# One loop instead of two: projections and linear attention by token tile, and norms by halves

## The reference

```python
mod = (silu(c) @ wmod)                      # sa, ca, ga, sb, cb, gb
h = layernorm(x) * (1 + ca) + sa
x = x + ga * attn(h)
h = layernorm(x) * (1 + cb) + sb
x = x + gb * ffn(h)
```

```python
q, k, v = x @ Wq.T + bq, x @ Wk.T + bk, x @ Wv.T + bv
g = sigmoid(x @ Wg.T + bg)
q, k = elu(rope(q)) + 1, elu(rope(k)) + 1
S = S + k_chunk.T @ v_chunk;  Z = Z + k_chunk.sum()
out = g * (q_chunk @ S) / (q_chunk @ Z + 1e-6);  y = out @ Wo.T + bo
```

## Time and profile before

| | |
|---|---|
| median of 3 runs | 743.06 us (739.28 to 743.28) |
| the profiled execution | 742.98 us |
| its span, first to last instruction | 741.2 us |
| mean granted TensorE clock | 0.92 of full |
| busy: TensorE, VectorE, ScalarE, GpSimd | 640.0, 478.9, 331.2, 167.9 us |

### The profile page before, as it was taken

One profiled execution on the slowest core, in us unless ns is written; L12 is line 12 of the kernel. 1 busy time (PEld: TensorE's weight loads), 2 busy tenths in 40 slices (PEclk: granted clock), 3 DMA queues, 4 the chain that ended last, 5 costly groups with the idle time before them and its releaser, 6 DMA issues.

```text
span 741.2 us, 10397 instructions
## 1 busy us (share of the span) xinstructions
PE 640.0 (86%) x3825; PEld 415.2 (56%) x3825; DVE 478.9 (65%) x982; ACT 331.2 (45%) x515; POOL 167.9 (23%) x206
## 2 busy tenths in 40 slices
PE   3948967999999959279999999668799999989996
PEld 3846746777777747135544433555454444358885
DVE  6894576777667469677888920476689888233333
ACT  5114043333333332405556676454265666844332
POOL 2451140555555309411000000000010001003222
PEclk9985586999999989569999999899899999999999
DMA  8720140000000000473100000016630000050001
GB/s 249 259 86 1 30 134 1 22 22 21 1 1 0 1 0 1 141 225 107 43 2 2 2 2 1 0 43 181 203 89 2 2 2 2 2 171 1 0 1 57
DMA packets 37182, 39.10 MB, mean 53 GB/s; under 512 B 4046, under 2 KB 36060, under 8 KB 36876
## 3 DMA queue, kind: packets, MB, share of 16 engines
q1 hardware_dynamic: 37132, 38.44, 16.8%
HBM read 30.89 MB, written 7.34 MB: 52 GB/s over the span
## 4 chain that ended last, share of the span: by engine, by line
PE 42%; issue 22%; DVE 12%; POOL 11%; SPq 5%; ACT 3%; DMA 3%; POOLq 0%; DVEq 0%; ACTq 0%
POOL it_lo L1534 8%; PE psum L732 8%; PE psum L695 8%; PE psum L718 8%; SPq L396 4%; DVE qk L1130 2%; POOL wd L1513 2%; PE psum L473 2%; PE psum L440 2%; PE psum L721 2%; DMA parts_scratch<-parts 2%; PE psum L442 2%; PE psum L441 2%; PE psum L698 1%; PE psum L544 1%
## 5 line engine op out<-in xcount | busy, mean ns | idle before, releaser
L908 ACT ACTIVATE pt<-psum 128x1024 f32<-128x1024 f32 (+1 forms) x192 | 148.1, 811 | 99.3 <-PE psum L721 71.0
L1214 DVE TENSOR_REDUCE mx<-psum 128x1 f32<-128x512 f32 (+3 forms) x216 | 132.4, 665 | 16.4 <-PE psum L695 8.3
L695 PE MATMUL psum<-kr,qr 96*128 96x512 bf16 (+3 forms) x384 | 112.1, 343 | 15.9 <-DMA kr<-parts_scratch 12.2
L718 PE MATMUL psum<-qr,kr 99*128 99x512 bf16 (+3 forms) x384 | 99.7, 333 | 7.6 <-DMA qr<-m3T 6.1
L1534 POOL TENSOR_TENSOR it_lo<-it,it_hi 128x512 fp32r<-128x512 f32 x48 | 67.2, 1401 | 156.8 <-ACT it_hi L952 156.8
L695 PEld LDWEIGHTS psum<-kr,qr 96*128 96x128 bf16 x384 | 37.4, 101 | 79.6 <-DVE mx L1214 29.4
L732 PE MATMUL psum<-pt,vp 128*32 128x512 f32 (+3 forms) x768 | 81.7, 498 | 0.0
L440 PE MATMUL psum<-h_hi,wf_hi 128*128 128x512 f32 x192 | 76.7, 399 | 2.7 <-issue 2.7
L441 PE MATMUL psum<-h_lo,wf_hi 128*128 128x512 f32 x192 | 75.8, 395 | 0.0
L442 PE MATMUL psum<-h_hi,wf_lo 128*128 128x512 f32 x192 | 75.7, 395 | 0.0
L952 ACT CAST it_hi<-it 128x512 fp32r<-128x512 f32 x48 | 29.8, 621 | 97.5 <-DVE it L1289 97.5
(11 more groups left out here) (189 smaller groups left out, 1098.0 us busy)
## 6 DMA issues: line engine op xcount, KB each, us to landing
parts_scratch<-parts SPq DMA_DIRECT2D x16, 384.0 KB, 3.5
qr<-parts_scratch SPq DMA_DIRECT2D x48, 128.0 KB, 2.6
kr<-parts_scratch SPq DMA_DIRECT2D x48, 128.0 KB, 2.7
wmod<-in_L_wmod SPq DMA_DIRECT2D x1, 1536.0 KB, 6.1
x<-in_L_attn_x SPq DMA_DIRECT2D x2, 512.0 KB, 4.0
wmod<-in_L_wmod SPq DMA_DIRECT2D x1, 1024.0 KB, 9.7
packed<-in_L_ffn_gate_W_packed SPq DMA_DIRECT2D x1, 1024.0 KB, 11.1
packed<-in_L_ffn_up_W_packed SPq DMA_DIRECT2D x1, 1024.0 KB, 12.9
```

The costliest lines, as they stand in the source:

```text
L695: m = pe.matmul(b, qr[0:PARTS_ROWS, c, h, (qt - 4 * c) * P:(qt - 4 * c + 1) * P], kr[0:PARTS_ROWS, ch, h, 0:w], start=True, stop=not diag)
L718: m = pe.matmul(bank[4 + 2 * at[0] + j][:, 0:w], kr[0:PARTS_ROWS + 3, kt // 4, h, (kt % 4) * P:(kt % 4 + 1) * P], qr[0:PARTS_ROWS + 3, c, ...
L908: act.activation(pt[:, n % 4, :, 0:w], psum[:, b:b + 2, 0:w], ACT.Exp, scale=0.25).then_inc(S["ex"], 1)
L1214: dve.tensor_reduce(dst, bank[at[0]][:, 0:k * w].rearrange("p (k w) -> p k w", k=k), AX, ALU.max).then_inc(S["p1_mx"], 1)
```

## The change

- The biases of the first layer's projections are laid in one row pair (high and low, partitions 0 and 32 of b0) and added by TensorE: one matmul with a constant operand of ones at the end of each group. ScalarE copies the results out of PSUM to qk, v1 and g. GpSimd prepares b0.
- The two loops become one of ten steps. Step s projects q and k of tile s, does the transposes and sums of tile s - 2, projects v and g of tile s, and closes with the product of tile s - 2. Key-value sums are made per tile, for the first 64 tokens (bank 2) and all 128 (bank 3), and the prefix is one multiply and one add for both. The sigmoid is taken in two parts, in steps 4 and 8. Gating on GpSimd begins in step 6.
- Transposes and output projection of the first 512 tokens stand in steps 8 and 9. The modulation columns are made in four groups; the last is put after the output projection of the second half.
- Norm, update, high and low are done by halves of 512 tokens in all four norms. In each engine's program, half 0's hT stands before half 1's root.
- The unpacking of the first two feed-forward weight tiles is put between the halves; the high and low parts of four second-layer weights move from the second loop into the first feed-forward, and their next load after the scales.

Its core:

```diff
+            for s in range(NT + 2):
+                t = s - 2
+                if s < NT:
+                    pe.wait_ge(S["ln_hl"], 2 * (s // 4) + 2)
+                    if s >= 2:
+                        pe.wait_ge(S["qk_b"], s - 1)
+                    token_major(s, bank[4 + 2 * (s % 2)][:, :], 0, 512, b0).then_inc(S["pj"], 1)
+                if s == NT:
+                    attention_transposes(0, 0)
+                    pe.wait_ge(S["ld_wmod1"], 16)
+                    pe.wait_ge(S["ca"], t)
+                    for j in range(6):
+                        m = modulation(wmod1, 1, 1, MOD1 + j, j)
+                    m.then_inc(S["mod_mm"], 1)
+                if t >= 0:
+                    q_transpose(t)
+                    kv_sums(t)
+                if s < NT:
...
+                    token_major(s, bank[5 + 2 * (s % 2)][:, :], 512, 1024, b0).then_inc(S["vj"], 1)
+                if s == NT:
+                    out_projection(0, 0, 0)
+                if s == NT + 1:
+                    out_projection(0, 0, 1)
...
+                if t >= 0:
+                    out_pair(t)
+            update(0, 0)
+            attention_transposes(0, 1)
+            for dt in range(KC):
+                pe.wait_ge(S["cu"], 8)
+                out_projection(0, 1, dt)
+            for j in range(6, 12):
+                m = modulation(wmod1, 1, 5, j, j)
+            m.then_inc(S["mod_mm"], 1)
+            update(0, 1)
...
@@ scalar
+            layer_norm_std(0, 0)
+            layer_norm_mod(0, 0)
+            layer_norm_std(0, 1)
             for i in range(4):
                 weight_hi(i, w_hi, i * D)
+            layer_norm_mod(0, 1)
...
             mlp_weights_hi(0, 0)
-            layer_norm_std(1)
-            layer_norm_mod(1)
+            for half in range(2):
+                layer_norm_std(1, half)
+                layer_norm_mod(1, half)
...
@@ vector
+            def prefix(t):
+                dve.wait_ge(S["kv"], t + 1)
...
+                dve.tensor_tensor(km[:, :, :, :] if t else cum[:, 0, :, :, :],
+                                  psum[:, 2:4, 0:2 * VW].rearrange("p r (f e) -> p r f e", f=2),
+                                  bd[:, :].unsqueeze(1).unsqueeze(1).to_broadcast([P, 2, 2, VW]), ALU.mult
+                                  ).then_inc(S["kmd" if t else "cu"], 1)
...
+            for s in range(NT + 2):
+                t = s - 2
+                if s < NT:
+                    rope_cos(0, s)
+                if 1 <= s <= NT:
+                    elu_add(s - 1)
+                if t >= 0:
+                    prefix(t)
+                if s < NT:
+                    rope_add(0, s)
+                if t >= 0:
+                    denominators(t)
+                    reciprocals(t)
+                    normalise(t)
...
             dequantise_bits(0)
             dequantise_value(0)
+            update(0, 1)
+            layer_norm(1, 0)
...
+            mlp_weights_lo(0, 0)
+            high_low(1, 0)
+            layer_norm(1, 1)
+            modulation_copy(3, 1, 5, 6, 6, 12)
             dequantise_bits(1)
+            high_low(1, 1)
             dequantise_value(1)
...
@@ vector, first feed-forward
                         (dequantise_bits, dequantise_value)[n % 2](n // 2 + 2)
+                    if f == 0 and n in (6, 8, 10):
+                        weight_lo(5 + (n - 6) // 2, (n - 6) // 2 * D)
@@ sync
-            sp.wait_ge(S["mod_mm"], 3)
+            sp.wait_ge(S["mod_mm"], 4)
             for j in range(FC[0] // 2):
```

More of the change, by code:

```diff
@@ L807, in _ @@
             mlp(1)
-            update(3)
+            for half in range(2):
+                update(3, half)
         @block.scalar
@@ L1015, in _ @@
             attention(1)
-            attention_out(2)
+            for half in range(2):
+                attention_out(2, half)
             mlp_weights_hi(1, 0)
@@ L1406, in _ @@
             attention(0)
[L1407 to L1408 removed]
+            for half in range(2):
+                update(2, half)
+                for v in range(2 * half, 2 * half + 2):
+                    layer_norm_stats(3, v)
+            for half in range(2):
+                layer_norm_var(3, half)
+                layer_norm(3, half)
             dve.wait_ge(S["ss_ok"], 8)
```

515 lines of the change are left out of this document (261 added, 254 removed).

## The result

The changed kernel took **774.4 us** (median of 4 runs, 767.27 to 779.89), against 741.17 for the kernel before on the same chip (4 runs, 738.5 to 743.28): a ratio of 1.042, 95% interval 1.033 to 1.051. It is slower, and by 27 us more than I forecast; the range (736 to 758) does not hold it. The profiled execution took 773.62 (span 771.7), the granted clock was 0.92 as before.

A forecast was written before the change was run, and what follows sets the result against it. VectorE was taken to bound the first loop and TensorE at half clock the second; layer one -2.4, feed-forward +1.8, norms +2.0 and +3.0 sum to +4.4 on 742.98, forecast 747.4 us, range 736 to 758.

The forecast's parts named there:

- TensorE's own work per step: Merged loop: projections, transposes, key-value sums and products at full clock add to 5.0 us a step, below the wait chain.
- The chain of 6.76 us: Merged loop: matmuls, ScalarE copy, VectorE rotation, ELU, prefix, product and handovers in series set each step, 6.76 us.
- The blocking: Merged loop: VectorE's ELU, now beside GpSimd's sine rotation, is slowed by 0.65 us a step.
- The rival of TensorE's pace: Merged loop runs at TensorE's 5.0 us a step: 10.6 us off, 736.8 us in all; chance 0.15.
- Step 8: Loop step with transposes, six modulation columns, sums, part of the output projection, product and waits: 7.7 us.
- The clock rival: TensorE's clock falls to 1.2 GHz from step 8 on, doubling its terms: +13.5, 760.9 us; chance 0.12.
- The tail: Loop's end to first down-projection: one serial chain through modulation columns, scale loads, norm and fill gives back 8.2 us.
- The head: Start to first projection: the norm by halves makes TensorE start 3.5 us later (bounds 0 to 4).
- Feed-forward +1.8: Feed-forward cycle: three low weight halves of 0.61 us enter it between bits and `it`, +1.8 us (bounds 0, 2.5).
- norm two +2.0: Layer two's first norm: projection waits for half 0's high-low behind half 1's norm on VectorE, +2.0 us (0 to 2.8).
- norm three +3.0: Last norm: all eight squares wait for the last hT, now later, +3.0 us (1 to 3.5).
- The rival that halved norms cost nothing: Norms two and three: half 0's work fills the wait, so no loss there; 742.4 us in all; chance 0.13.

The follow-up runs named there:

- the probe: Changed kernel with bias products over 128 rows and five of the six modulation columns of step 8 left out: 759.93 us, ratio 1.032.

## Why the prediction was wrong, step by step

**Where the 26 us went.** The forecast stood for a span of 745.6 us, the profile has 771.7. Of the difference 11.0 lie ahead of the loop's last product: 1.7 in the head, 2.1 from there to the end of the first tile's product, 2.1 in the five full steps (37.6 us, forecast 35.5), 4.4 in step 8 and 0.7 in step 9. 6.5 lie between there and the first down product, 8.6 behind it.

**TensorE's own work per step (5.0 us): the step that failed first.** It was 6.5. The sums, 0.95 by a price per column (bounds 0.6 to 1.3), cost 1.5: a pair of records takes 0.43 whether they have 64 rows or 128, and only 64-row products on different rows run beside each other. The bias products, 0.23 each, cost 0.42 each with 33 rows (0.8 more for the two groups of a step, with what they wait themselves), and 0.23 with 128. Undoing the two showed it: 0.74 us a step for the bias, 0.84 for the sums. And the modulation columns of steps 3 to 5, which I had hidden under waits, lay bare on an engine that never waited (0.95 to 1.43 us a step).

**The chain of 6.76 us.** Its terms add to 6.31 and not to 6.1 as written, so to 6.96 with the ELU's share. The blocking was right: the ELU took 1.32 us beside GpSimd's sine rotation in five of eight steps, and 0.68 to 0.73 in the others. Behind its table load (58.24 us, 1.28 long) step 5's exponential started at 59.53, with nothing between them. From ScalarE's copy to the end of the prefix addition the chain took 3.95 us (49.70 to 53.65), where the terms give 4.24 before handovers. It stood beside TensorE's work, not above it; it became the bound in the changed kernel's step with gating beside the prefix addition (1.32 us for 0.72, TensorE idle for 0.8 at 69.1 us), and in steps with gating and cheap sums. The rival of TensorE's pace had the right mechanism and the wrong price: with 6.5 of own work and up to 1.43 of modulation it ends on the slow side, and the sign that I gave for it, a step below 6.0, could not show it. At the upper end of my bound for the sums TensorE's work came to 5.4 us; the range could not reach the time measured, since its bounds came from the same prices.

**Step 8 (7.7 us, was 12.1).** The clock rival. Its reason against ("the clock fell before only in idle stretches") was true of the kernel before and no law. The clock's share of the 4.4 us is some 3.0, by the probe and the profiles beside it; the columns themselves were in the forecast. The other 1.4 are mostly the sums' price again, and 1.0 us in which TensorE waits for GpSimd's gated tile (77.3 to 78.3), of which I had 0.4 for all waits. The rival's own price, 13.5 us from step 8 on, was too high: the clock rose again at 88.2 us. A second low stretch cost the tail's output projection 1.8.

**The tail (+8.2, was +14.5).** Mechanism right in every link: scales behind the columns, the fill on the path. Undoing the order of the columns gave 10.7 us from the last product to the feed-forward, 6.1 of them net of what step 9 took on and of the clock: this link alone cost three quarters of what the whole tail had lost in my sum. Mis-sized: the output projection at the low clock (5.2 for 3.4), the landing (6.4 for 4.8), and the fill, which I had put on GpSimd's path alone, while it held VectorE's twelve-column instruction for 4.04 us ahead of `it`.

**The head (+3.5, was +5.2).** The norm by 512 tokens costs what I had: with GpSimd out of the way of the norm the first projection came at 22.0, 3.4 behind. The other 1.8 us are the bias preparation, whose instructions were not in my sum at all.

**Feed-forward +1.8, norm two +2.0, norm three +3.0.** Measured 1.2, 2.1, 4.2; the undoing of the last two gave back 2.5 and 4.3. For the feed-forward the forecast was 0.3, with the 1.5 that I had taken off for a better entry: that entry did not show. Norm three was low by the clock: the second pair of hT came 4.56 us behind the first where I had 4.3, and the four products of line 793 behind it took 3.42 us at the low clock, where they took 1.98 in the kernel before and 1.99 in the run with the roots together. So 1.4 of the 4.2 is the clock's, and the waits that I had summed are nearer to 2.8. The rival that halved norms cost nothing was wrong by both.

**Not in the forecast:** 1.4 us in layer two's attention and 5.0 behind the last norm. Behind the last norm the fifteen other profiles took 251.4 to 255.4 us (the middle one 253.1), the kernel before 251.5 in its only profile: since one kernel with the change took no longer than the kernel before, the change need not cost anything there, and what made the 5.0 stays open. In attention every kernel with the change took 0.5 to 3.2 us more than the kernel before; the cause stays open.

## What to carry to other kernels

Before a chain of waits is believed, add up the bound engine's own work with a measured pitch for every shape in it, at the rows and columns it will have; where a shape has no row in the trace, a price per column from another shape is no bound. When work is merged into a loop, everything that lay in idle time before (here modulation columns, a fill, a preparation on GpSimd) must be placed again, because the idle time is what the merge removes. Short instructions that prepare something are part of the change too: look at what each will stand beside on the other engine. And before a clock is read off a window, look whether the pitch of a dense product agrees with it.

## What the runs showed of the hardware

- A 33-row product between 128-row ones took 0.42 us, a 128-row one of the same columns 0.23. Its weight load started with its own product (34.72 us), that of the 128-row one with the product before (34.03 for 34.25). Zero rows are cheaper than missing ones.
- With TensorE busy, its granted clock fell to 0.5 while 24 one-column records ran (low from 81.3 to 88.2 us); with four such records in that place it stayed at 1.00, and so it did over the second 24 of the same kernel. It also fell in mid-loop with TensorE busy, for 3.4 to 17 us, in four of the eight profiles with 33-row products; no run shows why.
- At the start a dense product kept the pitch of 1.2 GHz, 0.43 us for 512 columns, up to 47 us in one execution and to 26 in two others of the same loop. The 1.00 that the windows print there stands for no clock record, not for full speed.
- GpSimd and VectorE hold each other, and the size of the instruction says little: twelve columns took 4.04 us beside a fill of 3.51, and GpSimd's 2.78 us became 8.62 beside VectorE's work. The Trainium skill, "SBUF — State Buffer", section on who interferes with whom, has the second instruction wait until the first finishes. The traces agree as to waiting, but the wait lasted over the other engine's whole unbroken run: VectorE's twelve columns started at 135.68 us beside the end of GpSimd's scaling (to 136.25) and ended at 139.72, with the fill that GpSimd began behind it (136.19 to 139.70). GpSimd's preparation ended 2.64 us behind a run of VectorE instructions that began ahead of it and went on for 6 us. The ELU's 1.32 us beside a sine rotation is 0.64 above its time alone, nearer to the 0.65 of my row than to the 0.84 of a whole GpSimd instruction.
